# Opening of a fused attention and FP4 feed-forward kernel: weights as one stream of twelve chunks

## The reference, cut to what matters

```python
# x, ctx: 32 x 256 x 512 float32
x = x + _L0_xattn_ref(_layernorm(x), ctx, ctx, Wt, Wp, Wg, Wz, gamma, beta)
x = x + _L0_ffn_ref(_layernorm(x), w_gate, w_up, w_down)

def fp4_quant_dequant(x):                       # last dim in blocks of 16
    scale = max(abs(block)) / 6.0, at least 1e-12
    idx = searchsorted(_MID, abs(block / scale))
    return _GRID[idx] * sign(block) * scale     # grid 0 .5 1 1.5 2 3 4 6
def fp4_linear(x, w):
    return einsum('bsk,nk->bsn', fp4_quant_dequant(x), fp4_quant_dequant(w))
def _L0_ffn_ref(x, w_gate, w_up, w_down):       # 1408x512, 1408x512, 512x1408
    h = silu(fp4_linear(x, w_gate)) * fp4_linear(x, w_up)
    return fp4_linear(h, w_down)
def _L0_xattn_ref(q, k, v, ...):                # 8 groups of 32 channels
    p, g, t = Wp q, Wg k, Wt v                  # over the 256 channels
    att = sum(p * g) * 0.125 per group; y = Wz (att * t)
    return groupnorm(y) * gamma + beta + v
```

## Time and profile before

| | us |
|---|---|
| median of 3 runs | 1893.15 (1892.28 to 1893.98) |
| the profiled execution | 1893.97, span 1892.2 |
| busy in the span: PE, DVE, ACT, POOL | 1742.4, 1656.3, 719.6, 805.8 |
| mean granted TensorE clock | 0.978 |

### The profile page before, as it was taken

One profiled execution on the slowest core, in us unless ns is written; L12 is line 12 of the kernel. 1 busy time (PEld: TensorE's weight loads), 2 busy tenths in 40 slices (PEclk: granted clock), 3 DMA queues, 4 the chain that ended last, 5 costly groups with the idle time before them and its releaser, 6 DMA issues.

```text
span 1892.2 us, 30546 instructions
## 1 busy us (share of the span) xinstructions
PE 1742.4 (92%) x10062; PEld 1098.9 (58%) x10062; DVE 1656.3 (88%) x2629; ACT 719.6 (38%) x1237; POOL 805.8 (43%) x1065
## 2 busy tenths in 40 slices
PE   1537999999999999999999999999999999999996
PEld 1436566666666666666566666666566666666653
DVE  5585999999999999999999999999999999999984
ACT  2334434333344343433344343433434333433431
POOL 3648434344444434344444434434344444434400
PEclk9778999999999999999999999999999999999998
DMA  5100232322322232323222233222232233232222
GB/s 192 53 1 17 44 70 69 75 60 61 72 69 63 60 69 70 74 60 68 64 69 70 54 69 75 69 67 68 58 74 70 56 67 69 69 73 61 48 54 47
DMA packets 281879, 123.04 MB, mean 65 GB/s; under 512 B 252928, under 2 KB 254208, under 8 KB 281856
## 3 DMA queue, kind: packets, MB, share of 16 engines
q1 hardware_dynamic: 281856, 122.74, 27.4%
HBM read 43.03 MB, written 16.78 MB: 32 GB/s over the span
## 4 chain that ended last, share of the span: by engine, by line
PE 40%; DVE 35%; issue 16%; ACT 5%; POOL 2%; DVEq 1%; DMA 1%; ACTq 0%; SPq 0%; POOLq 0%
PE pairs L463 19%; PE obank L474 13%; PE pairs L442 4%; DVE hq L759 3%; DVE q L785 3%; DVE h L751 3%; DVE h L916 3%; DVE h L742 3%; ACT early L711 3%; DVE h_amax L763 3%; PE ubank L442 2%; DVE x L814 1%; ACT u_dev L600 1%; DVE ln_st L818 1%; DVE xn L755 1%
## 5 line engine op out<-in xcount | busy, mean ns | idle before, releaser
L463 PE MATMUL pairs<-w_gate_hi,xT_parts 128*128 128x352 f16 x2048 | 629.3, 313 | 16.1 <-DVE h L916 11.7
L463 PE MATMUL pairs<-w_up_hi,xT_parts 128*128 128x352 f16 x2048 | 628.4, 313 | 0.0
L474 PE MATMUL obank<-w_parts,hT_parts 128*128 128x512 f16 x2112 | 468.0, 380 | 12.9 <-DMA hT_parts<-raw 12.9
L474 PEld LDWEIGHTS obank<-w_parts,hT_parts 128*128 128x128 f16 x2112 | 207.5, 100 | 249.3 <-issue 15.9
L463 PE MATMUL pairs<-w_up_lo,xT_parts 128*128 128x352 f16 x1024 | 320.4, 313 | 0.0
L463 PE MATMUL pairs<-w_gate_lo,xT_parts 128*128 128x352 f16 x1024 | 320.3, 313 | 0.0
L463 PEld LDWEIGHTS pairs<-w_gate_hi,xT_parts 128*128 128x128 f16 x2048 | 205.3, 100 | 142.5 <-DVE h L916 23.3
L463 PEld LDWEIGHTS pairs<-w_up_hi,xT_parts 128*128 128x128 f16 x2048 | 200.6, 98 | 97.5
L916 DVE SCALAR_TENSOR_TENSOR h<-pairs,w_unit,early 128x352 f32<-128x352 f32 x256 | 148.1, 579 | 91.0 <-ACT early L711 90.9
L711 ACT ACTIVATE early<-pairs,w_unit 128x352 f32<-128x352 f32 x256 | 141.0, 551 | 86.6 <-PE pairs L463 86.6
L625 ACT CAST raw<-hq 128x704 f16<-128x704 f32 x128 | 99.6, 780 | 183.0 <-DVE hq L759 181.6
(11 more groups left out here) (163 smaller groups left out, 3023.6 us busy)
## 6 DMA issues: line engine op xcount, KB each, us to landing
x_in<-in_x SPq DMA_DIRECT2D x32, 512.0 KB, 3.4
c_in<-in_ctx SPq DMA_DIRECT2D x32, 512.0 KB, 3.5
out<-early SPq DMA_DIRECT2D x64, 256.0 KB, 2.1
raw<-in_L_ffn_w_down SPq DMA_DIRECT2D x2, 1408.0 KB, 8.8
raw<-in_L_ffn_w_gate SPq DMA_DIRECT2D x2, 1280.0 KB, 8.4
w_parts<-in_L_ffn_w_up SPq DMA_DIRECT2D x2, 1280.0 KB, 9.1
xT_parts<-raw SPq DMA_TRANSPOSE x64, 3.1
hT_parts<-raw SPq DMA_TRANSPOSE x64, 5.2
```

Source lines behind the costliest of these rows:

```text
L463: mm = pe.matmul(pairs[:, pair, n, 0:GW], xT[s][part][:, k, :], w1[n][wpart][:, k, c * GW:(c + 1) * GW], start=(k == 0 and part == 0 and w ...
L474: mm = pe.matmul(obank[:, :], hT[part][:, k, :], w2[wpart][:, k, :], start=(k == 0 and part == 0 and wpart == 0), stop=(k == KH - 1 and pa ...
```

## The change

- Products and rounding happen in place in the staged weights; the three extra buffers are gone. The rounding's sum goes to a PSUM region of three banks, `w_sum`, made of the banks of `tbank` and `obank`; the second instruction reads it from there.
- The maximum over partitions is taken by TensorE: `top_of_rows` multiplies the row maxima with the identity into one row of PSUM, VectorE takes its maximum (`weight_top`), `spread_top` multiplies it back to all partitions.
- Scales and inverses are made for half a matrix at a time; the inverses' scaling by `SNAP_BELOW` moves to GpSimd, that of the scales to ScalarE (`scale_all`).
- Both turns of a set go to the same bank of `pairs[:, 1]`, alternating between two banks, and all 34 sets take the two turns. The scores and groups of the first two tiles use `pairs[:, 0]`, but for one group.
- The loops over phases and `body(0)` are replaced by lists of calls written out for each engine. The gate's and up's chunks come before the first group of `hidden`, most down chunks' turns between the groups of tiles 0 and 1, and the opening ends with `output(0)`. The loop body from tile 2 on has the same calls as before.

```diff
-            def all_max(m):
-                pool.wait_ge(w_rowmax_done, m + 1)
-                nc.gpsimd.partition_all_reduce(w_max[:, m, 1:2], w_max[:, m, 0:1], P, RMAX).then_inc(w_allmax_done, 1)
...
+            def top_of_rows(m):
+                pe.wait_ge(w_rowmax_done, m + 1)
+                at_least(pe, w_ready, m)
+                pe.matmul(ubank[0:1, P:2 * P], w_max[:, m:m + 1], ident[:, :], start=True,
+                          stop=True).then_inc(w_row_turned, 1)
+            def spread_top(m):
+                pe.wait_ge(w_top_done, m + 1)
+                pe.matmul(ubank[:, 2 * P:2 * P + 1], ones_row[:, :], w_top[:, m:m + 1], start=True,
+                          stop=True).then_inc(w_allmax_done, 1)
...
+            def weight_top(m):
+                dve.wait_ge(w_row_turned, m + 1)
+                nc.vector.tensor_reduce(w_top[:, m:m + 1], ubank[0:1, P:2 * P], AX_X, ALU.max).then_inc(w_top_done, 1)
...
-            def weight_steps(n):
...
+            def weight_round(n):
+                m, c = divmod(n, WCH)
+                dve.wait_ge(w_grain_done, n + 1)
+                at_least(dve, w_r_done, n)
+                nc.vector.scalar_tensor_tensor(out=w_sum, in0=wm[n % 2], scalar=GRAIN, in1=staged(m, c * H, H), op0=ALU.max,
+                                               op1=ALU.add).then_inc(w_t_done, 1)
+                dve.wait_ge(w_t_done, n + 1)
+                nc.vector.scalar_tensor_tensor(out=staged(m, c * H, H), in0=wm[n % 2], scalar=GRAIN, in1=w_sum, op0=ALU.max,
+                                               op1=ALU.subtract).then_inc(w_r_done, 1)
...
-                nc.gpsimd.tensor_tensor(wy[n % 3].rearrange("p (b e) -> p b e", e=BLK),
-                                        staged(m, c * H, H).rearrange("p (b e) -> p b e", e=BLK),
-                                        over_block(w_rinv[m % 2][:, c * HB:(c + 1) * HB]),
+                if n % 2 == 0:
+                    both = w_rinv[m % 2][:, c * HB:(c + 2) * HB]
+                    pool.wait_ge(w_inverse_done, n // 2 + 1)
+                    nc.gpsimd.tensor_scalar(both, both, SNAP_BELOW, None, ALU.mult).then_inc(w_rinv_done, 1)
+                pool.wait_ge(w_rinv_done, n // 2 + 1)
+                nc.gpsimd.tensor_tensor(blocks(staged(m, c * H, H)), blocks(staged(m, c * H, H)), over_block(rinv),
                                         ALU.mult).then_inc(w_y_done, 1)
...
-                    mm = pe.transpose(tbank[:, k % 2, c, :], staged(m, col, P), ident[:, :])
+                    mm = pe.transpose(pairs[:, 1, k % 2, c * P:(c + 1) * P], staged(m, col, P), ident[:, :])
...
+            def scale_all(m):
+                act.wait_ge(w_gain_done, m + 1)
+                act.wait_ge(w_rowmax_done, m + 1)
+                nc.scalar.activation(w_scale[m % 2][:, :], w_scale[m % 2][:, :], ACT.Identity,
+                                     scale=w_gain[:, m:m + 1]).then_inc(w_scaled, 1)
...
+                if isinstance(t, int) and t == 0:
+                    act.wait_ge(w_rest_done, sets_before(WCH))
...
+            pe.wait_ge(w_lo_done, ALL_SETS)
+            hidden(1, 1, 3)
+            output(0)
```

More of the change, by code:

```diff
@@ L457, in hidden @@
             def hidden(j, s, c):
[L459 removed]
+                pair = pair_of(j, s, c)
                 for k in range(KD):
@@ L523, in _ @@
             pe.wait_ge(minus_made, 1)
[L524 to L540, removed]
+            unit_read(0)
@@ new lines, in _ @@
+            scores(0, 0)
+            turn_weights(0)
+            turn_again(0)
+            turn_weights(1)
+            turn_weights(2)
+            turn_again(1)
+            turn_again(2)
+            group_means(0)
+            turn_weights(3)
+            turn_weights(4)
+            turn_again(3)
+            group_spread(0)
+            turn_weights(5)
+            top_of_rows(1)
+            turn_again(4)
+            spread_top(1)
+            turn_weights(6)
+            turn_again(5)
@@ L568, in body @@
                             group_spread(j + 2)
[L569 to L574, removed]
+                    output(j - 1)
             with pe.Fori(1, NB - 2) as i:
@@ L664, in _ @@
             ctx_hi(0)
-            q_hi(0)
[L666 to L678, removed]
-                for one, before in zip(sets + [None], [None] + sets):
-                    if one:
-                        weights_hi(one)
-                    if before:
-                        weights_lo(before)
-                if step == 2 and 0 <= t < HT:
-                    affine(t)
-                if n == 6:
-                    grain(xm[:, :], xn[:, :], x_y_done, 1, x_grain_done)
-                if n == 8:
-                    x_hi(0)
-                if n == 5:
-                    ctx_hi(1)
-                if n == 7:
-                    q_hi(1)
+            act.wait_ge(consts_made, 1)
@@ new lines, in _ @@
+            add_ctx(0)
+            ctx_lo(0)
+            weight_y(2)
+            q_lo(0)
+            weight_y(3)
+            weight_q(0)
+            weight_q(1)
+            weight_y(4)
+            weight_q(2)
+            pool.wait_ge(vectors_loaded, 32)
+            columns(0, 0)
+            weight_y(5)
+            columns_affine(0, 0)
+            weight_y(6)
+            weight_q(3)
+            ln1(1)
+            weight_q(4)
+            root2(0)
+            weight_q(5)
+            weight_q(6)
@@ new lines, in _ @@
+            columns(1, 1)
+            columns_affine(1, 1)
+            weight_y(7)
+            weight_y(8)
+            weight_y(9)
+            weight_q(7)
+            root2(1)
+            weight_y(10)
+            weight_q(8)
+            q_lo(1)
+            ctx_lo(1)
+            weight_q(9)
+            weight_y(11)
+            weight_q(10)
+            add_ctx(1)
+            columns(2, 0)
+            columns_affine(2, 0)
+            weight_q(11)
+            root2(2)
+            columns(3, 1)
@@ L1221, in body @@
+            columns_affine(3, 1)
+            ln1(2)
+            q_lo(2)
+            ctx_lo(2)
+            add_ctx(2)
+            root2(3)
             def body(i):
```

617 lines of the change are left out of this document (426 added, 191 removed).

## The result

The changed kernel takes 1830.58 us (median of 4 runs, 1829.30 to 1832.27), the kernel before 1893.39 in the same comparison: ratio 0.967 (95% interval 0.965 to 0.969). The forecast was 1835, range 1822 to 1858. The profiled execution took 1831.41 us, span 1829.6.

A forecast was written before the change was run, and what follows sets the result against it. GpSimd was taken to pace the opening. First group at 96 + 63.4 work + 5.4 waits put the first down product at 164.8 us, 58.8 earlier: 1893.97 - 58.8 = 1835.2, forecast 1835 us, range 1822 to 1858.

The forecast's parts named there:

- The loop carried over: From the first down product to the end: instructions and order unchanged, so 1668.6 us is carried over.
- First product on GpSimd: Start of the opening: GpSimd's first 128x1408 product starts at 14.1 us instead of 19.35.
- The holes are the all-reduce's: GpSimd in the opening: idle around three all-reduces, 41.1 us in all with the instructions, goes when TensorE takes the maximum.
- Rival 3: GpSimd's holes come back at another instruction: 41.1 us fewer gained, 1876 us (1857 if only the front ones); chance 0.04.
- From there to the first group: GpSimd's first product to first gate/up group: 57.7 us of GpSimd work times 1.36, then 3.3 us; group at 96.
- rival 5: Opening: the new order meets fewer locks, ratio 1.13 instead of 1.36, 13 us better, 1822 us; chance 0.08.
- rival 1: Opening's rounding: port takes both halves or the PSUM sum is slow, 22 us more, 1857 us; chance 0.12.
- From the first group to the first down product: End of the opening: TensorE's queue holds everything, 63.4 us of work plus 5.4 of waits, first down product at 164.8.
- Rival 2: Sets' turns, copies and written-out order sharing one pair of banks stall TensorE: +10 us, 1845 us; chance 0.16.
- TensorE's clock: First group to first down product: granted clock forecast near 1.0, with TensorE over 85% busy.
- rival 4: TensorE kept at 1.2 GHz through the opening's last stretch, doubling its 63.4 us: 1899 us; chance 0.05.
- The signs named: Profile after: no 6 us idle around GpSimd instructions, PSUM rounding half 1.6 to 1.7 us, first down product at 165.

The follow-up runs named there:

- experiment 1: Changed kernel with GpSimd's PARTITION_ALL_REDUCE put back three times in place of TensorE's maximum: 1861.98 us, +31.4 against the changed kernel.
- experiment 2: Kernel before with only TensorE's maximum over partitions, and VectorE's variance step moved ahead of it: 1858.51 us, -34.4 against 1892.91.
- experiment 4: Changed kernel with the sum between the rounding's two halves in SBUF instead of PSUM: 1841.34 us, +10.8.
- experiment 5: Changed kernel without the 44 products of the down weights' second turn on TensorE (9.8 us less work): 1830.96 us, +0.4.
- experiment 6: Changed kernel whose second half of the down weights' rounding writes one column instead of 1408 (6 us less on VectorE): 1830.48 us.
- experiment 8: Changed kernel without the down weights' second turn, their second rounding half one column, GpSimd's eight products on them 16 columns: 1826.21 us.
- 9a: Changed kernel with the up and down weights' scales reading a repeated constant column in PSUM through SCALAR_TENSOR_TENSOR: 1828.10 us, -2.5.
- experiment 7: Changed kernel without the down weights' second turn on TensorE and with one column in their second rounding half on VectorE: 1830.18 us.

## Why the prediction was right, step by step

- *The loop carried over:* forecast 1668.6 us from the first down product to the end, measured 1829.6 - 161.66 = 1667.9.
- *First product on GpSimd:* 14.1 forecast, 14.64 measured, 0.3 of the difference from one row: the 128x176 scaling that no row showed took 0.67 us, not 0.4.
- *The holes are the all-reduce's:* right, by experiments 1 and 2. Rival 3 is out. Taking out 41.1 us of holes brought 31 to 34.
- *From there to the first group:* forecast 96, measured 93.46. Chunk product 7 ended at 88.4, where I had 92.5: the list of 57.7 us took 73.8, a ratio of 1.28. I took 1.36, the page's rule alone gave 1.23, rival 5 had 1.13. That the half reading PSUM does not wait was right (experiment 4), and so rival 1 did not come. The reason given for the ratio holds only in part. Between 14.64 and 88.40 GpSimd is busy 61.9 us, 4.2 over its list; 10.4 us are five holes in which it waits for VectorE. The kernel before was alike: of the 35.1 us over its list 14.1 were longer instructions and 21.0 idle time. So the pace is not GpSimd's, as the prediction has it: VectorE is busy 71.2 of the 73.8 us. It waits inside its instructions, and not only in the rounding's first halves: a 128x176 scale, a normalisation of x and a pair for q each took over 2 us more than elsewhere. That 1.36 came near 1.28 is partly luck. The steps behind product 7 took 5.1 us, not 3.3, since ScalarE had three other instructions ahead of the grain. A second path to this place is not in the prediction: in experiments 5, 6, 8 and 9a TensorE waited there for the DMA that turns x (0.46 to 0.49 us).
- *From the first group to the first down product:* length right (68.8 forecast, 68.2 measured), reason wrong. The step said "Here TensorE's queue holds everything". The sum had 63.4 us of work and 5.4 of waits; measured are 65.6 busy and 2.6 idle, two misses that cancel. The chain of waits does run along TensorE from 116 us on, but with 9.8 us of its work gone nothing was gained (experiment 5), nor with 6 us of VectorE's gone as well (7); only less work on GpSimd shortened it (8), by 4 us for 20 taken out. So several chains end within a few us of each other, and VectorE's holds waits for GpSimd. I had the length right because I summed an engine that was indeed full, and because two misses cancel; that part is luck. As a statement of what to cut the step was misleading. Rival 2 (the two banks) did not come.
- *TensorE's clock:* 1.00 in the stretch, so rival 4 did not come. Its mechanism is seen at small size in experiment 5, where TensorE idled 9.4 us of the stretch.
- *The signs named:* all came, but one of them in the opening alone: idle times over 6 us on GpSimd remain in the loop (11.6 and 7.1 us), as waits for VectorE; the kernel's first down product came at 161.7, not 165.
- *The sum:* 3.1 us too late at the first down product, 0.7 in the loop: 1835.2 - 3.8 = 1831.4, the profiled execution.

## What to carry to other kernels

A full engine on the chain of waits isn't proof that its work is what holds the time: other chains can be as long, and only taking work out of the engine shows it. Here even work taken out of two engines brought nothing. Where a schedule is written out over four engines, look at the busy time of each beside its own list, since here about 12 of VectorE's 60 us were waits for GpSimd that the profile counts as busy. And ask of a slow collective what stands around it: 0.38 us of PARTITION_ALL_REDUCE cost 10 to 11.5 us each.

## What the runs showed of the hardware

- Each of three PARTITION_ALL_REDUCE had 5.8 to 6.6 us of nothing in front and 6.9 to 7.7 us behind, also the second and third time and in two different programs (the kernel before and experiment 1; behind the third one there, VectorE ended a rounding that GpSimd needed 0.6 us before the hole's end). The Trainium skill, GPSIMD Engine Reference (Instruction dispatch), tells of an instruction load of about 6 us at the first call of a freshly loaded kernel. The holes in front have that length, but at each of the three calls; that they, or the ones behind, are such loads is not shown.
- A TENSOR_SCALAR with its one input in SBUF waits for a running GpSimd product (0.24 to 2.43 us for 128x176); the same values through an instruction with one input repeated from a PSUM column did not (0.30 to 0.33 in all four, twice repeated). The wait is inside the duration of the instruction, not ahead of it. The Trainium skill, SBUF — State Buffer (Who interferes with whom), names tensor_scalar as one that can take the shared ports, beside the rule on two SBUF inputs that the prediction used; the trace agrees, and the prediction had left that half of it out.
- When one instruction was freed of its wait, part of it moved to the next with two SBUF inputs (3.39 instead of 2.74 us in 9a).
